# The seam from weight preparation to attention: the second token group's norm moved ahead of it, loads reordered

## The reference, cut to what matters

```python
x = x + L0_xattn(layernorm(x), ctx, ctx)     # 16 heads, softmax
x = x + L0_ffn(layernorm(x))                 # 512 -> 2048 -> 512, quantised to 8 bits
x = x + L1_xattn(layernorm(x), ctx, ctx)     # no softmax: collapses into one matrix per batch
x = x + L1_ffn(layernorm(x))                 # tanh(x W A1 A2 + b)
```

## Time and profile before

| what | us |
|---|---|
| median of 3 runs (1970.17 to 1971.45) | 1970.62 |
| the profiled execution | 1972.25 |
| its span, first to last instruction | 1970.2 |
| PE busy | 1862.2 |
| DVE busy | 1562.5 |
| ACT busy | 1243.6 |
| POOL busy | 959.0 |

### The profile page before, as it was taken

The page is one execution under the profiler, slowest core; times in us unless marked ns, Lnnn a source line. Parts: engine busy times, 40 slices in busy tenths (PEclk is TensorE's granted clock), DMA queues, the critical chain, the costliest instruction groups (busy, mean ns, idle before and its releaser), DMA issues. The chain is left out here.

```text
span 1970.2 us, 30832 instructions
## 1 busy us (share of the span) xinstructions
PE 1862.2 (95%) x9191; PEld 1356.0 (69%) x9274; DVE 1562.5 (79%) x3607; ACT 1243.6 (63%) x3379; POOL 959.0 (49%) x1055
## 2 busy tenths in 40 slices
PE   8995899999999999999977999979999999999997
PEld 7784677777777777877853444437677767767775
DVE  6755788888888888888765988887888888888874
ACT  4554888888887888888833334255655555655543
POOL 3122455555555565665540000036666666666664
PEclk9998999999999999999988999989999999999999
DMA  8375112222222112221129999635345445444411
GB/s 279 140 227 169 36 49 65 79 65 63 65 77 73 57 58 57 71 75 44 44 87 373 367 353 366 259 124 199 135 160 188 162 163 188 150 143 161 142 54 38
DMA packets 124679, 276.02 MB, mean 140 GB/s; under 512 B 41056, under 2 KB 51296, under 8 KB 106208
## 3 DMA queue, kind: packets, MB, share of 16 engines
q1 hardware_dynamic: 124368, 273.74, 40.7%
q10 hardware_dynamic: 144, 0.26, 0.1%
HBM read 165.95 MB, written 108.00 MB: 139 GB/s over the span
## 5 line engine op out<-in xcount | busy, mean ns | idle before, releaser
L1218 POOL TENSOR_TENSOR a_pr<-a_pr,a_rcp 128x512 f32<-128x512 f32 x256 | 266.5, 1041 | 332.6 <-DVE a_rcp L1061 332.6
L978 ACT ACTIVATE a_pr<-a_s,a_nmax 128x128 f32<-128x128 f32 x1024 | 362.4, 369 | 66.0 <-DVE a_nmax L1054 63.4
L1452 PE MATMUL f_pair<-f_room,w 128*128 128x512 bf16 x999 | 225.7, 383 | 12.3 <-DVE hmax L1679 9.8
L1054 DVE TENSOR_REDUCE a_nmax<-a_s 128x4 f32<-128x512 f32 x256 | 176.0, 688 | 65.8 <-PE a_s L60 61.8
L978 ACT ACTIVATION_READ_ACCUMULATOR a_pr<-a_s,a_nmax 128x1 f32 x1024 | 211.0, 206 | 0.0
L1679 DVE CUSTOM_DVE_ANT_0 f_hf<-f_pair,nb,sh 128x512 f32<-128x512 f32 x248 | 174.9, 749 | 40.0 <-PE f_pair L1452 25.6
L1899 POOL TENSOR_TENSOR f_ring<-f_ring,f_room 128x512 f32<-128x512 f32 x64 | 81.9, 1279 | 255.9 <-DVE f_room L1840 255.9
L1069 DVE TENSOR_TENSOR a_pTl<-a_pt,a_pTh 128x512 fp32r<-128x512 f32 x256 | 175.5, 685 | 35.5 <-ACT a_pTh L987 35.5
L1452 PEld LDWEIGHTS f_pair<-f_room,w 128*128 128x128 bf16 x1024 | 99.6, 99 | 127.0 <-DVE hmax L1679 10.3
L987 ACT ACTIVATE a_pTh<-a_pt 128x512 fp32r<-128x512 f32 x256 | 156.0, 610 | 30.4 <-PE a_pt L883 30.3
L1607 ACT ACTIVATE f_room<-f_ring,f_off,f_rs 128x512 f32<-128x512 f32 x128 | 103.9, 812 | 109.5 <-POOL f_off L1890 108.6
(11 more groups left out here) (400 smaller groups left out, 5227.3 us busy)
## 6 DMA issues: line engine op xcount, KB each, us to landing
hidden<-f_hf SPq DMA_DIRECT2D x58, 1024.0 KB, 7.5
f_hf<-hidden SPq DMA_DIRECT2D x58, 1024.0 KB, 5.3
xb<-x SPq DMA_DIRECT2D x16, 1024.0 KB, 5.4
a_xr<-x SPq DMA_DIRECT2D x64, 256.0 KB, 3.5
x<-a_xr SPq DMA_DIRECT2D x64, 256.0 KB, 2.0
f_ring<-x SPq DMA_DIRECT2D x64, 256.0 KB, 4.8
out<-f_ring SPq DMA_DIRECT2D x64, 256.0 KB, 4.5
f_room<-x SPq DMA_DIRECT2D x15, 1024.0 KB, 10.3
```

Of the source, the lines that this page charges most:

```text
L978: last = e.activation(pr[:, t, j, :], s_bank[t][:, j * P:j * P + P], ACT.Exp, bias=nmax[kk % 2][:, t, j:j + 1], accum_out=sums[kk % 2][:, ...
L1054: e.tensor_reduce(nmax[kk % 2][:, t, :], s_bank[t][:].rearrange("p (j n) -> p j n", j=4), AX, ALU.max, negate=True).then_inc(*e_max)
L1218: e.tensor_tensor(p, p, rcp[kk % 2][:, t, :].unsqueeze(2).to_broadcast([P, 4, KEYS]), ALU.mult).then_inc(*e_pn)
L1452: last = e.matmul(h_bank[(PAIRS * u + i) % 3][:, q, :], w1[:, k, f * P:f * P + P], xT[u % 2][:, k, :], start=k == 0, stop=k == KC - 1)
```

## The change

Five things change.

1. In `prepare`, the loads of token group 0 and of WT come directly after the last w2 rows, ahead of `send_m(3)`. The keys' first group comes later, after WqT.
2. Token group 1 is loaded before WoT (into `raw[0]`), and WoT goes into `raw[1]`, the buffer that WqT had. WoT's load is issued ahead of the last `send_w2`. The loads of groups 1 and 2 signal semaphores of attention (`X_LOAD`), so the end of `prepare` doesn't wait for them.
3. DVE also takes the statistics of group 1 (after the first low half of `wc`) and scales it (after the four halves of `x`). POOL raises both groups to the power -0.5, before it makes WoT's low half.
4. In attention the statistics and the scaling of group 1 are gone. Step 0 makes two chunks of its transposed tokens, steps 1 and 2 one each. The statistics of group 2 in step 0 stand at the step's end.
5. Early in `prepare`, the second `v1` bias and high half come before the split of weight 4.

```diff
...
                  w1_rows(0), w1_rows(1), w1_rows(2), w1_rows(3), w2_rows(0), w2_rows(1), w2_rows(2), plain("A1T"),
-                 plain("A2"), w2_rows(3), x_rows[0], plain("WT"), plain("WqT0"), plain("WoT0"), x_rows[1], x_rows[2]]
-        BUF = [i % 3 for i in range(20)] + [0, 0, 2]
-        W_LOAD, W_SLOT = (2, 3, 4, 5, 6, 14, 15, 18, 19, 20), (1, 2, 0, 1, 2, 0, 1, 2, 1, 0)
+                 plain("A2"), w2_rows(3), x_rows[0], plain("WT"), plain("WqT0"), x_rows[1], plain("WoT0"), x_rows[2]]
+        BUF = [i % 3 for i in range(20)] + [0, 1, 2]
+
+        X_LOAD = {20: scr["e_x"][1], 22: scr["e_x"][0]}
+        W_LOAD, W_SLOT = (2, 3, 4, 5, 6, 14, 15, 18, 19, 21), (1, 2, 0, 1, 2, 0, 1, 2, 1, 0)
...
             weight(3)
-            biased("v1", 2, 12, (0,))
+            biased("v1", 2, 12, (0, 1))
             weight(4)
-            biased("v1", 2, 12, (1, 2))
+            biased("v1", 2, 12, (2,))
...
+            for i in range(2):
+                halve("t", i, 16 + i, [x[:, i, :] for x in t1])
             e_raw[2].wait_ge(e, nth(17))
...
+            stats(0)
+            for i in range(2, KC):
                 halve("t", i, 16 + i, [x[:, i, :] for x in t1])
...
+            norm(0)
             p = place["row"][0]
             e_prod.wait_ge(e, p)
             e.tensor_copy(scr["sw2row"][:], bank[p % 6][:]).then_inc(*e_gone)
             weight(8)
+            scr["e_x"][1].wait_ge(e, 0)
             for i in range(KC):
+                if i == 1:
+                    stats(1)
                 if i == 2:
                     for k in range(KC):
                         halve("x", k, 22 + k, [x[:, k, :] for x in v1])
+                    norm(1)
                 halve("wc", i, 20 + i + KC * (i // 2), [x[:] for x in outs[i]])
...
             e_half.wait_ge(e, 0)
-            e_var.wait_ge(e, 0)
-            e.tensor_tensor(rs[:, 0:TPG], rs[:, 0:TPG], rs[:, TPG:2 * TPG], ALU.pow).then_inc(*e_rstd)
+            for g in range(2):
+                e_var.wait_ge(e, g)
+                e.tensor_tensor(rs[:, g, :], rs[:, g, :], half[:], ALU.pow).then_inc(*e_rstd)
             e_whi.wait_ge(e, 9)
-            e.tensor_tensor(slot[0][1][:], raw[BUF[20]][:], f32(slot[0][0][:]), ALU.subtract).then_inc(*e_wo)
+            e.tensor_tensor(slot[0][1][:], raw[BUF[W_LOAD[9]]][:], f32(slot[0][0][:]), ALU.subtract)
...
-            for i in (21, 22):
-                e_raw[BUF[i]].wait_ge(e, nth(i))
...
-        TURNED, ASKED = 4, 1
+        NORMED, TURNED, ASKED = 2, 4, 1
...
-                early = first(b) and kk < 3
-                if first(b) and kk == 0:
-
-                    stats(b, 4 - LN_A, LN_A, (0, 1), 0)
-                    stats(b, 4 - LN_B, LN_B, (2, 3), 1)
-                if not first(b) or kk >= 0:
+                opening = first(b) and kk == 0
+                if not opening:
                     stats(b, kk, LN_A, (0, 1), 0)
                     stats(b, kk, LN_B, (2, 3), 1)
                     norm(b, kk)
                 vsum(b, kk)
                 rc(b, kk, 2)
-                if not early:
+                if opening:
+                    xlo(b, -1)
+                elif not first(b) or kk > 0:
                     xlo(b, kk)
-                elif kk > 0:
-                    xlo(b, 2 * kk - 3)
                 plo(b, kk, 2)
                 smax(b, kk, 3)
                 plo(b, kk, 3)
-                if first(b) and kk == 0:
-                    norm(b, 4 - NORM)
-                if early and kk > 0:
-                    xlo(b, 2 * kk - 2)
+                if opening:
+                    xlo(b, 0)
+                    stats(b, kk, LN_A, (0, 1), 0)
                 x1_stats(b, kk)
```

More of the change, by code:

```diff
@@ L700, in _ @@
             load(16)
-            keys(0)
[L702 to L706, removed]
+            load(17)
+            load(18)
+            send_m(3)
+            send_w2(2)
+            load(19)
+            keys(0)
+            load(20)
             keys(1)
-            load(20)
             keys(2)
+            load(21)
+            send_w2(3)
             keys(3)
-            send_w2(3)
-            load(21)
+            load(22)
             for i in range(KC):
@@ L790, in attend @@
         e_kt, e_v = ([ev(f"{n}{c}", 128) for c in range(KC)] for n in ("keys", "values"))
-        e_x = [ev(f"xload{i}", 16) for i in range(2)]
+        e_x = scr["e_x"]
         e_xr = [ev(f"xagain{i}", 16) for i in range(4)]
@@ L891, in queries @@
                 if part == 0:
-                    if first(b) and o < 3:
-                        e_qlo.wait_ge(e, o - 1 - ASKED)
-                    elif first(b) and o == 3:
-                        e_xlo.wait_ge(e, 5 - TURNED)
-                    else:
+                    if not first(b) or o > ASKED:
                         e_xlo.wait_ge(e, (min(u + 3, NT - 1) if isinstance(u, int) else u + 3) - TURNED)
@@ L1025, in step @@
                 exp(b, kk, 2)
-                early = first(b) and kk < 3
-                if not early:
+                opening = first(b) and kk == 0
+                if opening:
+                    xhi(b, -1)
+                elif not first(b) or kk > 0:
                     xhi(b, kk)
-                elif kk > 0:
-                    xhi(b, 2 * kk - 3)
                 phi(b, kk, 2)
@@ L1033, in step @@
                 phi(b, kk, 3)
-                if early and kk > 0:
-                    xhi(b, 2 * kk - 2)
+                if opening:
+                    xhi(b, 0)
                 exp(b, kk, 3)
@@ L1147, in stats @@
                 last.then_inc(*e_bn)
[L1148 removed]
+                e_bn.wait_ge(e, 2 * (G - NORMED) + group)
                 e.memset(tick[:], 0.0)
@@ L1263, in step @@
                 prob(b, kk, 1)
-                if not first(b) or kk >= 0:
-                    rstd(b, kk)
+                rstd(b, kk)
                 prob(b, kk, 2)
-                if first(b) and kk == 0:
-                    rstd(b, 4 - LN_B)
                 clo(b, kk)
@@ L2045, in program @@
             scr["xb"] = [early.enter_context(nc.sbuf_tensor(f"xb{i}", [P, TPG, D], F32)) for i in range(2)]
+            scr["e_x"] = [Event(scr["sem"](f"xload{i}"), 16) for i in range(2)]
             kept = nc.snapshot_sems()
```

87 lines of the change are left out of this document (42 added, 45 removed).

## The result

The changed kernel takes 1969.05 us at the median of 18 runs (1964.14 to 1973.00), the kernel before 1972.47 at the median of 18 (1969.82 to 1974.47): ratio 0.9982, 95% interval 0.9975 to 0.9989, so 3.5 us (2.2 to 4.9) were won. The forecast was 5.5 us of gain. The time lies in its range, 0.5 us under the upper end, and the sign is right, but the gain is smaller. It is also under the 3.9 us (0.2%) that the prediction took as the bound between "faster", which it gave 0.66, and "same", which it gave 0.30: by its own bound the likelier of the two did not come. The second series can't be told from no change at all.

A forecast was written before the change was run, and what follows sets the result against it. TensorE is full from 57 to 148 and from 271 us, so the seam (148 to 223 us) has room. Seam 0.7 + attention 4.5 + early reorder 0.3 = 5.5 us off the 1970.62 median: 1965.1 us, range 1960.8 to 1969.6.

The forecast's parts named there:

- WT earlier: Start of the seam: ACT splits WT at 142.5, 5.7 us sooner; PE may start the wc products at 152.2, not 157.9.
- WoT late: Seam: WoT's load, sharing WqT's buffer, issues at 157.1 and lands at 162.8; PE's hole moves behind the second wc product.
- The second norm and the port: Seam: DVE's scaling of group 1 waits 2.7 us for POOL's low part of Wo, running from 174.8 to 176.7.
- a scaling that starts near 172 would prove the seam's term wrong: Sign in the changed profile: DVE's second scaling should start as POOL's Wo low part ends; near 172 would refute the seam.
- The end of the seam: Last wc store issued by 178.4, landing at 180.7 against 181.6: 0.9 us won, 0.7 with some play at the queue.
- Attention: First three attention steps: step 3 starts 35.8 us after the first product, against 40.5; 4.7 us won, 4.5 taken.
- Early reorder: Early in the first part: PE's fourth value product, which waited 1.70 us at 53.36, starts at once; 0.3 us won.
- No port wait: Rival at the seam: scaling runs beside POOL, stores end near 178, total 1962.4 us; chance 0.16.
- keys held back: Rival on the queue: first key copy held until WqT lands, WoT issued near 161.9, 4.8 us late; total 1969.9; chance 0.17.
- attention gives little: Rival in attention: step 0's chain through one bank costs what the statistics did, 1.5 us instead of 4.5; 1968.1; chance 0.07.
- slower: Rival on the queue: two key-copy groups each held 7.36 us, WoT lands at 175.5, 12.7 us late; 1977.8; chance 0.04.
- The forecast case: Whole kernel: seam, attention and early reorder together win 5.5 us, giving 1965.1; own range 1962.8 to 1967.5; chance 0.53.

The follow-up runs named there:

- wt_late: The changed kernel with WT's load behind the last m stores on the queue, as before the change; 1973.08 us, ratio 1.0008 to the kernel before.
- after_again: The changed kernel, unedited, measured again as the second series; 1970.58 us, ratio 0.9992 (0.9983 to 1.0001) to the kernel before.
- port: The changed kernel, with GpSimd's subtraction for Wo's low part waiting until VectorE has scaled the second token group; 1966.59 us, ratio 0.9966.
- x_last: wot_off_path with the load of the third token group behind the wc stores on the queue instead of ahead; 1961.86 us, ratio 0.9944.
- x_last_k3: x_last with the fourth group of key copies ahead of WoT's load on the queue; 1963.78 us, ratio 0.9955.
- after: The changed kernel as it stands, first series and first profile; 1969.05 us, ratio 0.9982 to the kernel before.
- wot_sooner: The changed kernel with WoT's load ahead of the third group of key copies instead of behind it; 1968.64 us, ratio 0.9979.
- stores_later: x_last without the first part's wait for the wc stores; their tiles are shared with attention, and ScalarE waits in step 5; 1958.79 us, ratio 0.9931.
- wot_off_path: The changed kernel with ScalarE splitting WoT behind its high half of the third wc product, not ahead of the first; 1965.08 us, ratio 0.9966.

## Why the prediction was right, and where it was not

*WT earlier: right.* ACT split WT at 141.85 (142.5 forecast), Wq's low part ended at 156.5 in the first profile and 155.9 in the second (157.0), and PE started `wc` at 151.59 (152.2). `wt_late` shows what it guards.

*WoT late: right in kind and nearly in size.* The hole stood where it was put, behind the second product. WoT was issued at 157.5 and landed at 163.4 in `after_again` (157.1 and 162.8 forecast); in the first profile it was 159.2 and 164.9, since the queue was 1.4 us later already when it issued the w2 store ahead of WqT (143.07 for 141.65). The keys were not held as in the rival that puts WoT at 161.9; holds of about 1 us are there.

*The second norm and the port: right.* In `after_again` Wo's low part ended at 175.3 and the scaling at 176.9 (174.8 and 176.7). One point of the forecast's list was loose: the scaling does not start as GpSimd ends, its first instruction starts at 172.48 and is held inside (3057 ns in the first profile). Taken by the letter, the prediction's sign "a scaling that starts near 172 would prove the seam's term wrong" came, although the wait that the term stands for was there; the sign was ill chosen, since the wait does not show as a late start. `port` settled it: 1.91 us without GpSimd beside it.

The Trainium skill (SBUF — State Buffer, "Who interferes with whom") gave the same rule, that the later of VectorE's two-port form and GpSimd waits for the whole instruction. The 4.43 and 1.91 us agree with it, and so does the subtraction from PSUM in `port` that kept its 0.69 us.

*The end of the seam: wrong, and this is the term that failed.* The sum was 0.7 us won; the three profiles give 1.8 us lost against the two of before, and this with the early reorder's 0.5 already in it. Up to the last store's issue the chain is only 0.5 us late (178.88 in `after_again`, 178.4 forecast). The failing step is "lands in 2.0 us on a quiet queue, four in a row in a little more": the last took 3.3 us where the sum had 2.3 (178.4 to 180.7), landing at 182.2. The price came from stores of `m_all`, issued mostly one at a time; the last four of `wc`, issued within 1.4 us, land 0.75 us apart on average (179.9 to 182.2), as the eight of `x_last` land 0.88 apart. Another 0.3 us is the handover from landing to first product (1.15 for 0.85). These three, 0.5 + 1.0 + 0.3 us, are the 1.8 us between the 0.9 us won of the forecast's chain and the 0.9 lost in `after_again`. And the profile of before on which the sum stood was 0.7 us later at this point than its second one (182.45, 181.74).

*Attention: right.* 4.5 us forecast, 3.9 measured over six steps by the means, with step 3 at 35.86, 35.45 and 35.80 us (35.8). The mark itself was a little generous: step 3 takes 12.7 us and not 11.94, with 1.53 us of idle at 223.18, so part of the 4.7 us at its start is given back in it. The split of the sum was off: VectorE's row gives some 3.7 of it and not 2.9.

*Early reorder: right,* 0.3 forecast, about 0.5 shown. The wait of 1.70 us is not saved but moved, as the forecast's 0 to 0.7 allowed.

*The rivals.* "No port wait", "keys held back", "attention gives little" and "slower" each named a mark, and none came. (The time itself, 1969.05, is nearer to the 1969.9 of "keys held back", but WoT was issued at 157.5 and 159.2 and not 161.9.) The forecast case held in its mechanism, with one term of wrong size: -5.5 became about -2 by the profiles, -3.5 and -1.6 by the two series. That the time fell inside the range is in part luck. The kernel before measured 1972.47 in the same series and not the 1970.62 that the forecast started from, and the case's own range, 1962.8 to 1967.5, does not hold 1969.05; less that shift of 1.85 us it would be 1967.2. And with the gain of the second series alone, 1.6 us, the forecast of 5.5 would be more than three times too large.

## What to carry to other kernels

Follow the end of a phase to the landing of its last store, and take that landing from stores that were issued in the same company: the last of four in a row took 3.3 us here, the last of eight 5.3 (5.4 with a megabyte in front), one alone 2.0. When a load becomes late, look at who stands behind it on the in-order engine that uses it: moving one split down ScalarE's list, one load behind the stores and one wait out of the seam took another 0.5% (0.9931 for 0.9982), more than the whole change. When a phase ends waiting only for stores, let the next phase own the memory and the wait.

## What the chip showed that was not expected

- A DMA issue directly behind a megabyte load and a w2 store (512 KB in small pieces), in this order, was held until that load had nearly landed (0.04 to 0.12 us before): 4.56 to 4.83 us for a key copy behind WoT and w2, in ten profiles, 4.84 us for a `wc` store in its place (`x_last_k3`), 5.26 us for the load of WqT behind WT and w2 (`wt_late`). The median issue took 0.42 us. The 7.36 us of the earlier trace rows fit it: there WqT and w2 were ahead, and the hold ended as WqT landed. So do the 3.75 to 4.50 us for which the second w2 store near 121.5 us is held behind the load of A and the first one, in all fourteen profiles. The order counts: with w2 first and WqT behind it (`after`), no key copy was held longer than 1.00 us before WqT landed at 152.24. Directly behind WoT alone, in `wot_sooner`, eight copies went out unheld, and only those behind w2 waited, 1.28 and 1.16 us. Why the pair holds the queue, no run shows.
- The eight stores of 256 KB landed 0.88 us apart on average, the last four of the changed kernel 0.75. A megabyte load took 5.1 to 11.1 us between 110 and 185 us, depending on what else was on the queue, WoT's 5.6 to 5.9.
- After 2.94 us of idle at the seam (`port`) PE's clock was full; around the first product behind 5.7 to 6.6 us of idle (`after`, `after_again`, `wot_sooner`, `wt_late`) it was at half for 6.8 us; behind 3.85 us (`stores_later`) for 3.4 us; behind 8.2 to 11.0 us (`x_last_k3`, `x_last`, `wot_off_path`) for 10.2 us. The length of the idle alone does not settle it: at the products with WT the clock was full behind 3.07 us (`after`) and at half behind 2.83 us (`after_again`).
- The time at the half clock between 400 and 1940 us is 41.0 to 47.8 us in the three profiles of the changed kernel, 41.0 in both of before, and up to 51.2 us over all fourteen. The stretches between 586 and 602 us follow idles of 1.87 to 2.24 us; idles of 1.57 to 1.98 us there passed without one in other profiles. The seam too varies, by up to 1.5 us (183.35 to 184.86), with how late the queue is.
